# Attention stage of a fused transformer kernel: K and Q packed through DRAM, another split of their conversion over the engines, an fp32 output projection, and another order of the loads

## The reference, cut to what matters

```
q = (layernorm(x) @ Wq + bq)   16 heads of 16 channels
k, v = ctx @ Wk + bk, ctx @ Wv + bv
attn = softmax(clip(q k^T / 4, -1e4, 1e4))
x = x + (attn v) @ Wo + bo
```

## Time and profile before

| | us |
|---|---|
| median of 3 runs | 1246.32 |
| lowest, highest | 1243.24, 1253.02 |
| the profiled execution | 1251.51 |
| its span, first to last instruction | 1249.7 |

### The profile page before, as it was taken

How to read it: one execution, slowest core, us unless ns; L and a number is a source line. 1 busy time by engine, 2 the same in 40 slices (tenths; PEclk the granted TensorE clock), 3 DMA queues, 4 the chain that set the end, 5 groups by cost and what they waited for, 6 DMA issues and landing times.

```text
span 1249.7 us, 22415 instructions
## 1 busy us (share of the span) xinstructions
PE 892.6 (71%) x7878; PEld 660.1 (53%) x7878; DVE 737.3 (59%) x1388; ACT 564.2 (45%) x1159; POOL 313.7 (25%) x269
## 2 busy tenths in 40 slices
PE   4756777877788548539899999335249895649996
PEld 2434555655566435427567777211037773548885
DVE  8646575665576577418567675136886666791224
ACT  2334454444454226314455554259845554831222
POOL 3247565555564113640000000460000000110000
PEclk9978789788798666859999999656667877868999
DMA  5453444446633324413357461650000000020001
GB/s 128 98 109 93 106 112 105 105 117 118 121 80 78 93 69 143 125 47 103 106 155 206 150 197 32 150 121 0 2 6 1 1 0 1 1 67 2 0 0 53
DMA packets 83125, 99.94 MB, mean 80 GB/s; under 512 B 25484, under 2 KB 65983, under 8 KB 82984
## 3 DMA queue, kind: packets, MB, share of 16 engines
q1 hardware_dynamic: 77492, 90.36, 28.8%
q0 software_dynamic: 4096, 6.57, 2.1%
q10 hardware_dynamic: 1476, 2.20, 0.6%
HBM read 74.10 MB, written 13.32 MB: 70 GB/s over the span
## 4 chain that ended last, share of the span: by engine, by line
PE 42%; DVE 16%; SPq 10%; DMA 9%; issue 8%; ACT 7%; POOL 3%; another core or an unknown queue 3%; ACTq 1%; DVEq 0%; POOLq 0%
PE ps L1126 8%; PE ps L1113 7%; DMA qs<-mTl 5%; SPq L436 4%; PE ps L1912 4%; SPq L433 3%; PE ps L1900 3%; PE ps L1634 3%; PE ps L544 2%; PE ps L1580 2%; PE ps L377 2%; PE ps L1623 2%; ACT area L1746 2%; PE ps L578 1%
## 5 line engine op out<-in xcount | busy, mean ns | idle before, releaser
L531 DVE TENSOR_REDUCE m<-ps 100x2 f32<-100x722 f32 x128 | 114.6, 899 | 112.9 <-PE ps L526 112.0
L551 ACT ACTIVATE p<-ps 121x600 f32<-121x600 f32 x128 | 85.6, 668 | 107.3 <-PE ps L544 105.6
L544 PE MATMUL ps<-qs,ks 128*121 128x100 f16 x768 | 77.5, 246 | 69.9 <-DMA qs<-mTl 64.0
L1471 POOL PARTITION_ALL_REDUCE gmax<-cmax x6 | 6.2, 1041 | 466.2 <-DVE cmax L1466 466.2
L1175 ACT ACTIVATE hT<-ps,cols 128x500 f32<-128x500 f32 (+1 forms) x96 | 62.5, 651 | 133.7 <-PE ps L1113 123.9
L544 PEld LDWEIGHTS ps<-qs,ks 128*121 128x121 f16 x768 | 69.3, 162 | 88.6 <-DMA qs<-mTl 46.1
L1126 PE MATMUL ps<-w_h,hT_h 128*125 128x256 f16 (+1 forms) x384 | 104.7, 273 | 2.6 <-DVE x L1221 1.2
L1126 PE MATMUL ps<-w_h,hT_l 128*125 128x256 f16 (+1 forms) x384 | 104.7, 273 | 0.2 <-issue 0.2
L1126 PE MATMUL ps<-w_l,hT_h 128*125 128x256 f16 (+1 forms) x384 | 104.7, 273 | 0.0
L566 DVE SCALAR_TENSOR_TENSOR p<-p,xe 121x600 f32<-121x600 f32 x128 | 102.0, 798 | 2.6 <-DMA xe<-floor 2.6
L1182 DVE TENSOR_TENSOR hT_l<-hT,hT_h 128x500 f16<-128x500 f32 (+1 forms) x96 | 61.3, 641 | 66.3 <-ACT hT_h L1176 62.1
(11 more groups left out here) (347 smaller groups left out, 2387.6 us busy)
## 6 DMA issues: line engine op xcount, KB each, us to landing
xe<-floor SPq DMA_DIRECT2D x32, 378.1 KB
ks<-kp SPq DMA_DIRECT2D x96, 90.8 KB
sw<-in_L_ffn_w_dram SPq DMA_DIRECT2D x16, 512.0 KB, 7.3
sw<-in_L_ffn_w_dram SPq DMA_DIRECT2D x8, 1024.0 KB, 5.7
stage<-in_L_xattn_W_f_dram SPq DMA_DIRECT2D x6, 1024.0 KB, 9.0
ctx_f<-in_ctxT_dram SPq DMA_DIRECT2D x16, 270.8 KB, 5.8
stage<-in_ctxT_dram SPq DMA_DIRECT2D x8, 541.5 KB, 8.3
area<-in_ctxT_dram SPq DMA_DIRECT2D x4, 1083.0 KB, 7.3
```

Of the source, the lines that this page charges most:

```text
L531: v.tensor_reduce(m32[p][:, 2 * i:2 * i + 2], ps[0:T, at:at + 2, 0:KV], AX.X, ALU.max).then_inc(m_max, 1)
L544: mm = pe.matmul(bank[t_bank(i) + n][0:KT, j * T:(j + 1) * T], ks[p][:, h, j * KT:(j + 1) * KT], qs[p][:, h, :], start=(j == 0), stop=True ...
L551: s.activation(p32[:, i % HALF, :, :, :].rearrange("p j n t -> p n j t"), ps[0:KT, t_bank(i):t_bank(i) + 2, 0:KJ * T].rearrange("p n (j t) ...
```

## The change

1. **K and Q through DRAM.** `k_store` stores both parts of one half of K (256 runs of 726 bytes) to a DRAM buffer `k_parts`, and `q_store` both parts of Q (2 DMAs, 256 runs of 200 bytes each) to `q_parts`. `half_load` then reads them back with whole rows: for K 32 and 16 rows of 5808 bytes, for Q 16 and 34 rows of 1600 bytes. The 34 rows hold the second high part, the low part and two rows of zeros for the maxima, which makes the DMA from `zeros` go away: 4 issues for a half in place of 7, and 2 stores for Q and 1 for each half of K. `half_load` waits for the stores (`k_out`, `q_out`), a store waits for the last load of its buffer.
2. **Parts of K.** The high part of K is now a copy on ACT (`k_high`, behind the exponentials of steps 2 and 6); POOL has the subtraction alone. On POOL Q's parts stand at step 1 (before: step 2), K's low parts at steps 3 and 7 (before: 2 and 6). The low part of the context is split in two instructions (steps 5 and 6, before: 7), and ACT's high part of it stands at steps 4 and 5 (before: 6 and 7).
3. **Output projection.** `on32` is used in fp32 with the unscaled fp32 weights: 4 matmuls for a batch in place of 12; `oh_scalar`, `ol_gpsimd`, `last_scalar` and the split of Wo at the start are gone.
4. **SP's order.** `ROW_M` is 48. The rows of maxima of the second half stand ahead of the floor's store; those of the first half of b+1 stand ahead of the load of K and Q of b+2, and `inv_store` ahead of both. The store of K's second half of b+2 ends the call.

```diff
         def k_gpsimd(g, b, t, p, c):
...
-            g.tensor_tensor(kp[:, 0, c, 0:KV], k32[c][:, :], ones_col.broadcast_to((128, KV)), ALU.mult).then_inc(k_h, 1)
+        def k_high(s, b, c):
+            s.wait_ge(k_32, 2 * b + c + 1)
+            wait(s, k_out, 16 * (2 * b + c - 1))
+            s.copy(kp[:, 0, c, 0:KV], k32[c][:, :]).then_inc(k_h, 1)
+
+        def k_gpsimd(g, b, c):
             g.wait_ge(k_h, 2 * b + c + 1)
             g.tensor_tensor(kp[:, 1, c, 0:KV], k32[c][:, :], kp[:, 0, c, 0:KV], ALU.subtract).then_inc(k_l, 1)
+
+        def k_store(sp, b, t, p, c):
+
+            sp.wait_ge(k_l, 2 * b + c + 1)
+            wait(sp, (kq_in, k1_in)[c][p], 64 * t)
+            wait(sp, k_out, 16 * (2 * b + c))
+            sp.dma_start(k_d[p, c].rearrange("n p k -> p n k"), kp[:, :, c, :]).then_inc(k_out, 16)
...
+        def q_store(sp, b, t, p):
+
+            sp.wait_ge(q_l, b + 1)
+            for half in (kq_in, k1_in):
+                wait(sp, half[p], 64 * t)
+            wait(sp, q_out, 32 * b)
+            for c in range(CC):
+                sp.dma_start(q_d[p, c, 0:2 * 128].rearrange("(n p) t -> p n t", n=2), qp[:, :, c, :]).then_inc(q_out, 16)
...
-            for n, part in enumerate((0, 1, 0)):
-                sp.dma_start(ks[p][n * D:(n + 1) * D, heads, :], kp[:, part, c, :]).then_inc(done, 16)
-            sp.wait_ge(q_l, b + 1)
-            for n, part in enumerate((0, 0, 1)):
-                sp.dma_start(qs[p][n * D:(n + 1) * D, heads, :], qp[:, part, c, :]).then_inc(done, 16)
...
+            sp.wait_ge(k_out, 16 * (2 * b + c + 1))
+            k_hl = k_d[p, c].rearrange("n (d h) k -> (n d) (h k)", h=NP)
+            sp.dma_start(ks[p][0:2 * D, heads, :].rearrange("p h k -> p (h k)"), k_hl).then_inc(done, 16)
+            sp.dma_start(ks[p][2 * D:3 * D, heads, :].rearrange("p h k -> p (h k)"), k_hl[0:D]).then_inc(done, 16)
+            sp.wait_ge(q_out, 32 * (b + 1))
+            q_hl0 = q_d[p, c].rearrange("(r h) t -> r (h t)", h=NP)
+            sp.dma_start(qs[p][0:D, heads, :].rearrange("p h t -> p (h t)"), q_hl0[0:D]).then_inc(done, 16)
+            sp.dma_start(qs[p][D:ROW_M + 2, heads, :].rearrange("p h t -> p (h t)"), q_hl0).then_inc(done, 16)
...
             for k in range(HG):
-                for i, w in TERMS:
-                    mm = pe.matmul(UB_[0:T, 0:C], op[i][:, k, :], wo[w][:, k, :], start=(n == 0),
-                                   stop=(n == 3 * HG - 1))
-                    n += 1
+                mm = pe.matmul(UB_[0:T, 0:C], on32[:, k * T:(k + 1) * T], w_in_["Wo_heads"][0][:, k, :], start=(k == 0),
+                               stop=(k == HG - 1))
```

More of the change, by code:

```diff
@@ L787, in a_sync @@
                 wait(sp, a_s, NP * b)
-                half_load(sp, b + 1, t + p, q, 1, b >= 1)
+                half_load(sp, b + 1, q, 1)
             if has(b, 4):
                 context_load(sp, b + 4, p)
+            rows_load(sp, b, p, 1)
             floor_store(sp, b, 1)
-            rows_load(sp, b, p, 1)
+            if has(b, 2):
+                q_store(sp, b + 2, t + 1, p)
             floor_load(sp, b, 1)
@@ L796, in a_sync @@
             if has(b, 2):
[L797 to L801 removed]
+                k_store(sp, b + 2, t + 1, p, 0)
             if b >= 1:
@@ L804, in a_sync @@
             if has(b, 1):
-                floor_load(sp, b + 1, 0)
+                rows_load(sp, b + 1, q, 0)
+                floor_store(sp, b + 1, 0)
+            if has(b, 2):
+                sp.wait_ge(a_s, NP * b + HALF)
+                half_load(sp, b + 2, p, 0)
             if b >= 1:
                 inv_load(sp, b - 1)
+            if has(b, 1):
+                floor_load(sp, b + 1, 0)
+            if has(b, 2):
+                k_store(sp, b + 2, t + 1, p, 1)
             if has(b, 1) and not has(b, 2):
@@ L847, in last_vector @@
                 v.reciprocal(rden[:, n], bank[0][:, n]).then_inc(o_r, 1)
-                if k == 1:
-                    y_vector(v, b - 1)
+            y_vector(v, b - 1)
+            for k in range(HG):
+                n = slice(k * T, (k + 1) * T)
                 v.wait_ge(o_r, b + k + 1)
                 v.tensor_tensor(on32[:, n], o32[b % 2][:, n], rden[:, n], ALU.mult).then_inc(o_n, 1)
-                if k >= 1:
-                    low(k - 1)
-            low(HG - 1)
         def guard_sums_tensor(pe, free):
@@ L2083, in _ @@
             g.wait_ge(a_pad, 1)
-            c_gpsimd(g, 0, 0)
+            for c in range(2):
+                c_gpsimd(g, 0, 0, c)
             for c in range(CC):
-                k_gpsimd(g, 0, 0, 0, c)
-            c_gpsimd(g, 1, 1)
-            q_gpsimd(g, 0, 0, 0)
+                k_gpsimd(g, 0, c)
+            for c in range(2):
+                c_gpsimd(g, 1, 1, c)
+            q_gpsimd(g, 0)
             g.memset(zeros[:, :, :], 0.0)
@@ L2092, in _ @@
             for c in range(CC):
-                k_gpsimd(g, 1, 0, 1, c)
-            q_gpsimd(g, 1, 0, 1)
-            c_gpsimd(g, 2, 0)
+                k_gpsimd(g, 1, c)
+            q_gpsimd(g, 1)
+            for c in range(2):
+                c_gpsimd(g, 2, 0, c)
             m_gpsimd(g, 0, 0)
@@ L2348, in head_picker @@
 def head_picker(np):
-    c = np.zeros((128 - 48, H * KP), np.float16)
-    c[64 - 48:] = -1.0
-    return c
+    return np.full((128 - 48, H * KP), -1.0, np.float16)
 _TRANSPOSED = ["L1_xattn_W_d2v", "L1_xattn_W_img", "L1_xattn_W_txt", "L1_xattn_W_att0", "L1_xattn_W_att1",
```

139 lines of the change are left out of this document (55 added, 84 removed).

## The result

| | before | changed |
|---|---|---|
| median, us | 1247.43 | 1261.59 |
| lowest, highest | 1243.24, 1253.02 | 1255.35, 1263.06 |
| runs | 4 | 4 |
| the profiled execution | 1251.51 | 1255.35 |
| its span | 1249.7 | 1253.5 |

The changed kernel takes 1.0112 of the time before, with a 95% interval of 1.0075 to 1.015: 14 us longer. The forecast was 1268, and 22 us longer.

A forecast was written before the change was run, and what follows sets the result against it. No engine is full; SP's queued transfers and the round trips it waits out bind the loop. 20 us in batches with zeros, 2 in the others and 0 elsewhere made 1246.3 + 22 = 1268 us, range 1208 to 1288.

The forecast's parts named there:

- the slower case: Whole kernel: the forecast itself, slower by 15 to 32 us, chance 0.42.
- The signs that it named: PE's step 4 waits 4 us and more for `mTl`; SP stands for DVE and K's store; batches 25 to 27 us.
- Stretch A: SP, second-half floor load to K's first-half loads: 7.5 us for 8.17, with SP waiting for DVE's inversion at 4.78.
- Stretch B: SP, first-half K loads to next second-half floor load: 15.36 us plus 3.1 for 2.0 of added mean DMA work, 18.5.
- The wait for K's store: `half_load` on SP's queue: store and landing add nothing to the 3.1 us while zeros are queued.
- The batch: Attention loop: 26.0 us for 23.5 in 8 batches with zeros, +20 us; other five 0.4 each, +2.
- POOL, ACT, start: POOL's relief and ACT's copies cost nothing, neither being full; the start ahead of the loop 0, within 2 us.
- Projection: PE ahead of step 7: +0.5 us a batch, hidden by the wait at step 4; end 0, within 1.
- The two rules: Runs under 512 bytes, 5 us over the loop, and transfer width, about 8 us higher; both left out of the sum.
- Rival 1: Step 4: the queue absorbs the work, PE's 2.9 us wait goes, 1201 us; chance 0.30.
- Rival 2: A wash: added work falls in gaps, B + 0.7 and A - 0.7, 1240 to 1252 us; chance 0.18.
- Rival 3: Round trips bind in every batch, the wait for K's store costing +4 in each: 1298 us; chance 0.10.

The follow-up runs named there:

- b_order: Kernel before with the changed kernel's SP order and nothing else, no packing through DRAM: 1.0542 of the kernel before.
- b_wide2: Kernel before with zeros stored from 128 partitions and the inverses' load in four DMAs: 1215.8 us, 0.9718 of the kernel before.
- a_kfirst: Changed kernel with the store of K's second half ahead of the inverses' and the floor's load: 1.0314 of the kernel before.
- after_again: The changed kernel, unaltered, measured a second time beside other runs: 1265.2 us, 1.0145 of the kernel before.
- b_fp32: Kernel before with only the changed kernel's fp32 output projection, split of Wo at the start kept: 0.9964 of the kernel before.
- a_inv4: Changed kernel with the inverses' load split into four DMAs of 32 partitions each: 1.0004 of the kernel before.
- a_wide3_den: Changed kernel with zeros from 128 partitions, inverses' load in four DMAs, Q's 34 rows in two, denominators' load moved up: 1216.3 us, 0.9741 of before.
- a_wide3: Changed kernel with zeros from 128 partitions, inverses' load in four DMAs, Q's 34 rows in two: 0.9948 of the kernel before.

## Why the prediction was right, and where it was wrong

**The sum.** The forecast was +22 us, measured +14 and +18: the first is just under the 15 to 32 that it gave the slower case, the second inside. The sign and the mechanism (B gets K and Q of the first half at its head, ends with landings, and the gain in A doesn't pay for it) held. The signs that it named came too: PE's wait for `mTl` is 4.75 us a batch, and SP stands for DVE and for K's store. The size came out right partly by luck, since errors cancelled inside B.

**Stretch A, 7.5 forecast, 6.32 measured.** The term that failed is the round trip of the denominators, 4.78 us, taken from a batch in which seven loads were issued behind it. Now one store is, and DVE inverts at 275.31, 3.72 us after the floor's load. b_order shows that this is the order's doing: with K's loads moved away from behind it the same load lands in 3.4 us in place of 4.6. b_wide2 shows it within one kernel: where K's loads follow 0.7 us behind, it lands in 4.5 to 4.7 us, and where SP waits and they follow 1.6 to 2.7 us behind, in 3.3 to 3.5. "The queue is drained in order" was thus too simple: here transfers issued later slowed the ones ahead of them.

**Stretch B, 18.5 forecast, 18.23 measured: the right number for the wrong reason.** The forecast took 2.0 us of added mean work for the loads and K's store, priced them at 3.1, and said that nothing comes off for SP's faster issue. In fact the order alone adds 6.0, of which 3.7 are SP's issuing ahead of the inverses' load and 2.3 are transfers; the rest of the change takes 3.0 of the issuing away again. Mean work in B grew by 1.5, not by 2.0. What was not seen is that B begins to count at the inverses' load: it runs on few engines, the zeros behind it do too, and what delayed its issue delayed the rows (a_kfirst, b_order).

**The wait for K's store.** That neither the store nor its landing "adds to the 3.1" was right, against the look of the chain, in which it has 7.10 us. a_kfirst takes five of its six microseconds away and gains nothing behind the inverses' load.

**The batch.** 26.0 forecast in batches with zeros, 24.55 in the one shown and 24.8 in the mean, for 23.3 before; batches 1 to 9 took 10.4 us more (9.0 in after_again), not 20. The later six took 4.1 us more (6.9 in after_again), not 2, over a time before that may be some us high (b_fp32). In them too narrow transfers count: with the inverses' load alone split (a_inv4) these six take 134.2 us, for 138.9 and 141.7 in the changed kernel and 134.8 before.

**POOL, ACT, start.** No run isolates POOL's relief. Before, SP waited for its parts of K two times in six batches, 0.6 us in all, so there was little to gain, as forecast. The loop begins at 55.2 us for 57.5, 56.9 in after_again, about the 2 us allowed.

**Projection.** Eight records of 4 fp32 matmuls take from 278.23 to 280.04:

```profile
278.23 1.97 PE L635 MATMUL ps<-Wo_heads_f,on 128*100 128x256 f32 x8 [0.20 <-ACT k L387]
280.04 0.49 PE L559 MATMUL ps<-qs,ks 128*121 128x100 f16 x6
```

1.81 us in place of 1.35, the 0.5 that was forecast, and b_fp32 shows that the loop hides it. The end got 1.2 us shorter (b_fp32) where 0 within 1 was said.

**The two rules.** The prediction left the width of transfers out of the sum and put its worth at 8 us, for Q's new load. Width was worth more than that: widening the zeros gives 1.2 to 1.3 us a cycle in either kernel, the inverses 1.2, Q's 34 rows 0.6 to 0.7. But zeros and inverses are as narrow before as now, so they don't explain why the changed kernel is slower. Only Q's load of 34 rows is new, and its 9 us, near the 8, are a part of the 14 to 18. The Trainium skill, DMA: Bandwidth & Descriptors (Why a DMA increments its semaphore by 16 and not by 1), says that a DMA runs on the largest number up to 16 that divides the outer dimensions of both its sides; by that the zeros ran on 5 engines, the inverses on 4 and the 34 rows on 2. The traces agree: besides one event near the issue, the zeros' store has five landing events and the inverses' load four, and the zeros have sixteen once they come from 128 partitions; the three splits agree too. The rule on runs under 512 bytes was not tested by a run of its own; the prediction's 5 us for it had no working, and Q's stores of 200-byte runs are in the changed kernel's time either way.

**Rivals.** Rival 1 (1201) fell: PE's wait at step 4 grew. The widened kernel (a_wide3_den) comes near what it described, a cycle of 21.4 us, but with four edits more. Rival 2's wash wasn't reached, though the gain in A was larger than forecast, 1.85 us for 0.7. Rival 3 priced K's store as a wait; it had 1298 us, and a_kfirst took the wait away without a gain.

## What to carry to other kernels

Look first at how many engines each transfer on a shared queue runs on, and give its outer dimension a multiple of 16 rows; here two such edits took 31 us off the kernel before, where the whole change cost 14 to 18. A long landing in the chain of waits tells where the queue is late, not which transfer makes it late: shift the transfer that the chain names and see whether the interval behind it moves. And price a new order and a new transfer apart: here the order alone cost 5.4% and the rest of the change gave back most of it. Neither number can be read from the 1.1% of the two together.

## What the runs showed that was not expected

- Transfers were slowed by those issued behind them, as they were by those ahead. The denominators' load lands in 3.4 us with one store or nothing behind it (changed, b_order) and in 4.6 with seven loads behind it (before). But with one store behind it and Q's stores and the floor's load close ahead it takes 5.0 (a_wide3), and 1.8 once it is issued ahead of these (a_wide3_den). The zeros land in 12.0 to 12.5 us where K's loads follow within 2 us (b_order, a_kfirst), and in 10.4 to 10.5 where these come over 6 us later (changed, after_again). Before, K's loads follow at once too and the zeros land in 9.9, but less lies ahead of them.
- With the inverses and the zeros wide, 500 KB of zeros land in 3.5 us (b_wide2), where they took 9.9.
- The inverses' load is cheaper in four pieces than in one, even with 1.1 us more of issuing on SP (a_inv4).
